# A two-layer MoE and ternary-FFN kernel on one Trainium2 core: rounding of the second layer's weights and the collect tables moved to GpSimd, VectorE's chains issued step by step

## The reference, cut to what matters

```python
def reference(x, ...):                       # x: 128 x 32 x 256, taken as 4096 tokens of 256
    h = x W^T + (x A_b^T) B_b^T * s_b        # adapter b chosen for each sample of 32 tokens
    scores = sigmoid(h gate_w^T)             # 8 experts, the two best of each token
    routed = sum over both: expert(h * score), expert(v) = (silu(v w1^T) * (v w3^T)) w2^T
    x = x + routed + shared expert(h)
    y = per-sample 32 x 32 mix of x          # a weight gathered by a condition index
    z = hbitlinear(relu(hbitlinear(y, w_up))^2, w_down)
    return x + z
# hbitlinear(v, w): v by a Walsh-Hadamard transform, rounded to 8 bits by row;
# w rounded to -1, 0, 1 times s, where s is the mean of |w|
```

## Time and profile before

| | us |
|---|---|
| median of 3 runs | 354.83 (352.88 to 356.35) |
| the profiled execution, its time | 355.2 |
| its span, first to last instruction | 353.4 |
| PE busy | 320.1 (91%) |
| DVE busy | 277.7 (79%) |
| ACT busy | 224.3 (63%) |
| POOL busy | 207.7 (59%) |

### The profile page before, as it was taken

How to read it: one execution, slowest core, us unless ns; L and a number is a source line. 1 busy time by engine, 2 the same in 40 slices (tenths; PEclk the granted TensorE clock), 3 DMA queues, 4 the chain that set the end, 5 groups by cost and what they waited for, 6 DMA issues and landing times.

```text
span 353.4 us, 8743 instructions
## 1 busy us (share of the span) xinstructions
PE 320.1 (91%) x2564; PEld 296.6 (84%) x2564; DVE 277.7 (79%) x732; ACT 224.3 (63%) x529; POOL 207.7 (59%) x211
## 2 busy tenths in 40 slices
PE   7999999799998999699999998999996889997785
PEld 6799988699888999598999988999985878885684
DVE  2788899988998888986545458778969898886796
ACT  4664331323445375457776767899788697896793
POOL 1100889889998899900002878888548888884000
PEclk9999999699999999999999999999999999999999
DMA  6982559162287578458497996868947458574004
GB/s 190 376 286 86 167 203 304 66 204 72 77 256 227 163 261 272 154 154 254 147 287 244 220 253 110 174 119 174 205 99 130 68 77 165 93 125 89 2 1 150
DMA packets 54092, 59.23 MB, mean 168 GB/s; under 512 B 9888, under 2 KB 48032, under 8 KB 54048
## 3 DMA queue, kind: packets, MB, share of 16 engines
q1 hardware_dynamic: 41040, 41.01, 37.9%
q0 software_dynamic: 12432, 17.57, 24.1%
q10 hardware_dynamic: 576, 0.10, 0.2%
HBM read 33.06 MB, written 25.59 MB: 166 GB/s over the span
## 4 chain that ended last, share of the span: by engine, by line
PE 30%; issue 11%; POOL 7%; DVE 7%; ACT 4%; DMA 2%; ACTq 0%; POOLq 0%; DVEq 0%
PE UP L1295 9%; POOL X L1395 7%; PE DN L1349 5%; PE TR L1262 3%; PE LB L1647 2%; PE HT L1327 2%; PE AUX L1647 1%; DMA X<-ys,POSY 1%; PE AUX L1461 1%; PE AUX L1506 1%; DVE XSL L1280 1%; DVE ST L1655 1%; PE UP L868 1%; PE AUX L1585 1%; ACT YS L1360 1%
## 5 line engine op out<-in xcount | busy, mean ns | idle before, releaser
L1395 POOL DMA_INDIRECT X<-ys,POSY x64 | 103.0, 1610 | 69.5 <-DMA ys<-YS 49.5
L1043 POOL DMA_INDIRECT hs<-ZF,POS x64 | 66.5, 1038 | 10.5 <-issue 9.9
L1042 POOL MEMSET PACE<- 128x512 f32 x64 | 35.1, 548 | 21.1 <-DVE POS L1031 21.0
L1295 PE MATMUL UP<-WH,XSH 128*128 x142 | 43.2, 304 | 0.5 <-issue 0.5
L1295 PE MATMUL UP<-WH,XSL 128*128 x142 | 39.9, 281 | 0.0
L1295 PE MATMUL UP<-WL,XSH 128*128 x142 | 39.8, 280 | 0.0
L1280 DVE TENSOR_TENSOR XSL<-TR,XSH 128x512 fp32r<-128x512 f32 (+1 forms) x36 | 24.4, 679 | 12.9 <-ACT XSH L1275 12.6
L1309 ACT ACTIVATE T<-UP,SCOL 128x128 f32<-128x128 f32 x71 | 22.4, 370 | 10.4 <-PE UP L1295 8.0
L1295 PEld LDWEIGHTS UP<-WH,XSH 128*128 128x128 f32 x142 | 26.8, 188 | 1.9 <-issue 1.3
L809 PE MATMUL AUX<-WH,ZR 128*128 128x264 f32 x128 | 26.6, 302 | 1.7 <-ACT ZF L832 1.1
L1275 ACT ACTIVATE XSH<-TR 128x512 fp32r<-128x512 f32 (+1 forms) x36 | 21.3, 592 | 8.9 <-PE TR L1262 8.5
(11 more groups left out here) (327 smaller groups left out, 999.1 us busy)
## 6 DMA issues: line engine op xcount, KB each, us to landing
ys<-YS SPq DMA_DIRECT2D x42, 256.0 KB, 3.4
XIN<-hs SPq DMA_DIRECT2D x71, 132.0 KB
X<-in_x SPq DMA_DIRECT2D x8, 512.0 KB, 6.8
out<-X SPq DMA_DIRECT2D x16, 256.0 KB, 2.9
X<-in_WE SPq DMA_DIRECT2D x8, 384.0 KB, 9.6
ZF<-in_xT SPq DMA_DIRECT2D x4, 512.0 KB, 4.4
XR<-in_xT SPq DMA_DIRECT2D x4, 512.0 KB, 7.9
hs<-ZERO SPq DMA_DIRECT2D x8, 132.0 KB
```

Of the source, the lines that this page charges most:

```text
L1042: e.memset(PACE[:, :], 0.0).then_inc(S["pac"], 1)
L1043: e.indirect_dma_start(hs, bass.IndirectOffsetOnAxis(ap=POS[:, k, t0 + t:t0 + t + 1], axis=0), HT[:, slot + t, :], None).then_inc(s_st[b % ...
L1295: mm = e.matmul(UP[s % 2][:, c * 256:c * 256 + 256], v[:, r % 2, k, c * P:(c + 1) * P], w[:, cols], start=(n == 0), stop=(n == 5))
L1395: e.indirect_dma_start(X1[:, tt, :], None, ys[p], bass.IndirectOffsetOnAxis(ap=POSY[:, k, tt:tt + 1], axis=0), compute_op=ALU.add).then_in ...
```

## The change

Four things are changed.

1. **Rounding on GpSimd.** `ternary` leaves VectorE. Its six steps on 128x1024 are cut in halves, which gives twelve steps on 128x512, and these stand in place of twelve of GpSimd's `PACE` memsets, at scatters 16 to 27. The four tiny steps stay on VectorE as `scales`. Loads and copies that reuse the weights' tiles wait for twelve steps, not six.
2. **Collect tables on GpSimd.** `home` leaves VectorE for GpSimd, after the last scatter, and its comparison is written with subtract, add, max and min, its sum over 16 columns with four halving adds. The first collect waits for both tables.
3. **Single steps.** VectorE's chains (`nonzero`, `sigmoid`, `top1`, `top2`, `place`, `first_count` and so on, `stats1`, `stats2`) are no longer one piece each but one piece a step: each step waits for what it reads, and `TIME` may set other work between them.
4. **Loads.** The constants come in one DMA, the condition indices on SP, `RAWB` after the adapter indices, and some loads of `x` and of expert weights later.

`TIME` is new throughout, for example:

```diff
-    "collect": [
-        183.4459, 185.3059, 187.1659, 192.7459, 196.4659, 200.1859, 202.0459, 209.4859, 211.3459, 213.2059,
+    "collect": [
+        177.6604, 179.5204, 181.3804, 186.9604, 190.6804, 194.4004, 196.2604, 198.1204, 207.4204, 209.2804,
```

The core of the rest:

```diff
+TERNARY_AT = 16
...
-            n = 0
-            for raw, q, c in ((WUR, WU, 4), (WDR, WD, 5)):
+        def ternary(e, i):
+            raw = (XFLAT[:, 0:2 * HID], YFLAT)[i // 2 % 2][:, i % 2 * HID:i % 2 * HID + HID]
+            q = (WU[:, :, :], WD[:, :, :])[i // 2 % 2].rearrange("p a b -> p (a b)")[:, i % 2 * HID:i % 2 * HID + HID]
+            c = 4 + i // 2 % 2
+            if i < 4:
+                e.wait_ge(S["sw"], 2)
                 e.tensor_scalar(raw, raw, SW[:, c:c + 1], MAGIC, ALU.mult, ALU.add).then_inc(S["wt"], 1)
-                e.wait_ge(S["wt"], n + 1)
+            elif i < 8:
+                e.wait_ge(S["wt"], i - 3)
                 e.tensor_scalar(raw, raw, MAGIC, 1.0, ALU.subtract, ALU.min).then_inc(S["wt"], 1)
-                e.wait_ge(S["wt"], n + 2)
-                e.tensor_scalar(q[:, :, :], raw, -1.0, None, ALU.max).then_inc(S["wt"], 1)
-                n += 3
-        at("vector", "ternary", 0, ternary)
+            else:
+                e.wait_ge(S["wt"], i - 3)
+                e.tensor_scalar(q, raw, -1.0, None, ALU.max).then_inc(S["wt"], 1)
...
             def scatter(e, t, k):
...
-                if k_th > 0:
-                    e.wait_ge(S["pac"], k_th)
-                e.memset(PACE[:, :], 0.0).then_inc(S["pac"], 1)
+                if TERNARY_AT <= k_th < TERNARY_AT + 12:
+                    ternary(e, k_th - TERNARY_AT)
+                else:
+                    cleared = k_th - (12 if k_th > TERNARY_AT else 0)
+                    if cleared > 0:
+                        e.wait_ge(S["pac"], cleared)
+                    e.memset(PACE[:, :], 0.0).then_inc(S["pac"], 1)
...
             def home(e):
+                e.wait_ge(S["pl"], 6 * GROUPS_OF[SEGMENTS[p]])
+                e.wait_ge(S["pt"], LINES_DONE[p])
+                e.wait_ge(S["pac"], 8 * NBLK - 12)
...
-                over = OVER[:, 0:2 * NE * n].rearrange("p (t i) -> p t i", i=2 * NE)
+                over = PACE[:, :].rearrange("p (k t i) -> p k t i", k=2, i=2 * NE)
+                for k in range(2):
+                    link(e, e.tensor_tensor(over[:, k], POSF[:, k, lo:hi].unsqueeze(2).broadcast_to([P, n, 2 * NE]), edge,
+                                            ALU.subtract))
+                link(e, e.tensor_scalar(PACE[:, :], PACE[:, :], 1.0, 0.0, ALU.add, ALU.max))
+                link(e, e.tensor_scalar(PACE[:, :], PACE[:, :], 1.0, None, ALU.min))
                 for k in range(2):
-                    link(e, e.tensor_tensor(over, edge, POSF[:, k, lo:hi].unsqueeze(2).broadcast_to([P, n, 2 * NE]), ALU.is_le))
-                    link(e, e.tensor_tensor(over, over, step, ALU.mult))
-                    link(e, e.tensor_reduce(SUMS[:, k, 0:n], over, AX.X, ALU.add))
-                e.tensor_tensor(POSY[:, :, lo:hi], POSF[:, :, lo:hi], SUMS[:, :, 0:n], ALU.add).then_inc(S["hom"], 1)
-            at("vector", "home", p, home)
+                    link(e, e.tensor_tensor(over[:, k], over[:, k], step, ALU.mult))
+                flat = PACE[:, :].rearrange("p (t i) -> p t i", i=2 * NE)
+                for w in (8, 4, 2, 1):
+                    link(e, e.tensor_tensor(flat[:, :, 0:w], flat[:, :, 0:w], flat[:, :, w:2 * w], ALU.add))
+                link(e, e.tensor_tensor(SUMS[:, :, 0:n], POSF[:, :, lo:hi], over[:, :, :, 0], ALU.add))
+                e.tensor_copy(POSY[:, :, lo:hi], SUMS[:, :, 0:n]).then_inc(S["hom"], 1)
+            at("gpsimd", "home", p, home)
...
                         if t == 0:
-                            e.wait_ge(S["hom"], p + 1)
+                            e.wait_ge(S["hom"], PARTS)
...
-            at("vector", "stats1", b, stats1)
+            for i in range(3):
+                at("vector", "stats1", b, lambda e, i=i: stats1(e, i), i)
```

More of the change, by code:

```diff
@@ new lines, in plan_route, with pick @@
+            for i in range(4):
+                at("vector", "sigmoid", g, lambda e, i=i: sigmoid(e, i), i)
+            def pick(e, j, sc, base, i):
+                e.wait_ge(S["gch"], before + 6 + 6 * j + i)
+                if i == 0:
+                    ins = e.tensor_reduce(g4(2 * j), r(sc), AX.X, ALU.max)
+                elif i == 1:
+                    ins = e.tensor_tensor(r(base), r(sc), c(2 * j), ALU.is_equal)
+                elif i == 2:
+                    ins = e.tensor_tensor(r(base + 1), r(base), w8, ALU.mult)
+                elif i == 3:
+                    ins = e.tensor_reduce(g4(2 * j + 1), r(base + 1), AX.X, ALU.max)
+                elif i == 4:
+                    ins = e.tensor_tensor(r(base + 2), r(base + 1), c(2 * j + 1), ALU.is_equal)
+                elif j == 0:
+                    ins = e.scalar_tensor_tensor(out=f(7), in0=f(6), scalar=-4.0, in1=f(3), op0=ALU.mult, op1=ALU.add)
+                else:
+                    ins = e.tensor_tensor(MCB[:, cols], f(6), f(10), ALU.add)
+                ins.then_inc(S["gch"], 1)
@@ new lines, in adapter_moe_quant_ffn, with whole, running @@
+        LINES_DONE = [COUNT_0 + STEPS_C * i + 11 for i in range(PARTS)]
+        HOME_LINKS = [16 * i for i in range(PARTS)]
+        def whole(e, i, out, rows, bias):
+            if i == 0:
+                return e.tensor_scalar(SM[:, 4, :], rows, bias, 1.0 / P, ALU.add, ALU.mult)
+            if i == 1:
+                return e.tensor_scalar(SM[:, 5, :], SM[:, 4, :], MAGIC, None, ALU.add)
+            return e.tensor_scalar(out, SM[:, 5, :], MAGIC, float(P), ALU.subtract, ALU.mult)
+        def running(e, i, length, k):
+            if i == 0:
+                return e.tensor_copy(PB[:, k, 0, NE:2 * NE], length)
+            d = (1, 2, 4)[i - 1]
+            return e.tensor_tensor(PB[:, k, i, NE:2 * NE], PB[:, k, i - 1, NE:2 * NE], PB[:, k, i - 1, NE - d:2 * NE - d],
+                                   ALU.add)
@@ new lines, in plan_first, with first_tables @@
+            for i in range(10):
+                at("vector", "first_count", 0, lambda e, i=i: first_count(e, i), i)
+            def first_tables(e, i):
+                if i < 4:
+                    e.wait_ge(S["pt"], 10 + i)
+                    spread(e, i, PARTS, n, filled[:, NE:2 * NE], jump).then_inc(S["pt"], 1)
+                else:
+                    tables(e, i - 4, 14, 0, n, EXF[:, PARTS, 0:n], ROWF[:, PARTS, 0:n], line[:, 0:1])
+            for i in range(9):
+                at("vector", "first_tables", 0, lambda e, i=i: first_tables(e, i), i)
@@ L1166, in plan_segment @@
[L1166 to L1175 removed]
+                e.tensor_copy(TAIL[:, :], end).then_inc(S["tl"], 1)
@@ new lines, in plan_segment, with last_tables @@
+            for i in range(7):
+                at("vector", "jumps", c, lambda e, i=i: jumps(e, i), i)
+            def last_tables(e, i):
+                number, rows, part, digit = EXF[:, 0, 0:n], ROWF[:, 0, 0:n], EXF[:, PARTS + 1, 0:n], EXF[:, PARTS + 2, 0:n]
+                first = COUNT_0 + STEPS_C * PARTS
+                if i < 4:
+                    e.wait_ge(S["pt"], first + i)
+                if i == 0:
+                    e.tensor_scalar(part, EXF[:, 0, 0:n], float(NE), -float(NE), ALU.is_ge, ALU.mult).then_inc(S["pt"], 1)
+                elif i == 1:
+                    e.tensor_tensor(digit, part, EXF[:, 1, 0:n], ALU.add).then_inc(S["pt"], 1)
+                elif i == 2:
+                    e.tensor_tensor(number, number, digit, ALU.add).then_inc(S["pt"], 1)
+                elif i == 3:
+                    e.tensor_tensor(rows, rows, ROWF[:, 1, 0:n], ALU.add).then_inc(S["pt"], 1)
+                else:
+                    tables(e, i - 4, first + 4, 1, n, number, rows, LINE[:, 0, 0:1])
@@ L1176, in plan_segment @@
             if c == PARTS - 1:
-                at("vector", "last_tables", 0, last_tables)
+                for i in range(9):
+                    at("vector", "last_tables", 0, lambda e, i=i: last_tables(e, i), i)
             def tails(e):
```

539 lines of the change are left out of this document (296 added, 243 removed), and 258 rows, old and new, of the table TIME.

## The result

The changed kernel takes **362.64 us** (median of 4 runs, 362.03 to 365.26) against 354.4 us (352.88 to 356.35): a ratio of **1.0244**, 95% interval 1.0172 to 1.0315. It is slower by 8.2 us. 357.8 was forecast, 0.8% slower than before, with a range of 349.3 to 363.3: the time lies inside the range, near its upper end and near the time of rival B (362.3). The profiled execution has a span of 360.0 us, 6.6 us more than before.

What follows compares the result with a forecast made beforehand. Phase 2's start was taken to bound the kernel. The scatter chain gains 3.3 us and pays S = 10.5; phase 2 starts 4.8 us later with 1.8 us less work: +3.0, 358.2 profiled, 357.8 us median, range 349.3 to 363.3.

Steps and rivals of the forecast that it cites:

- rival B: GpSimd's queue becomes the bound: reload and fillers delay scatters, last scatter gates phase 2; S = 15, 362.3 us; chance 0.35.
- Phase 2's start sets the time: From phase 2's first transpose to the last pair TensorE is busy 95.1 of 98.6 us, so its start sets the time.
- Part 1: VectorE without rounding: 5.9 us leave ahead of group 2's chain; TensorE and ScalarE reach block 7 5.8 us earlier, at 97.1.
- The chain's gain of 3.3 us: GpSimd's scatter chain: 2.0 us of rounding's delay and 1.27 us of waits for POS go away.
- L, the reload: GpSimd library reload ahead of the first rounding step: 6 us, ends 0 and 9.6.
- F, the dearer filler: Rounding steps in GpSimd's fillers cost 0.29 us more than a memset, times 12: 3.5 us, ends 0 and 5.
- C: Clashes of GpSimd's new fillers with VectorE: three of a third of a microsecond, 1 us; ends 0 and 3.
- S: Price paid by the scatter chain, L + F + C = 10.5 us, ends 0 and 17.6; the end shifts by S - 7.5.
- Where S goes: ScalarE waits about 7 us at block 7; phase 2's loads, at 163.2, come last, behind TensorE's 158.5 or 161.9.
- A: Rival: the reload on GpSimd is cheap, S = 3, shift -4.5, 350.3 us; sign: gap on GpSimd missing; chance 0.20.
- Part 3: Collect tables on GpSimd after the last filler: 0, with a cover of 35 us before the first collect.
- Part 4: Single steps and loads: 0, with -1 to +1 in the last 32 us, behind the last collect.

Runs made afterwards that it cites:

- forms: round_on_vector with twelve different GpSimd steps on 128x512 in place of the memsets at scatters 16 to 27; mult and add took 0.63 us, others 1.53 to 2.34.
- steps_alone: Changed kernel with rounding and collect tables both back on VectorE, single steps and new order kept: 362.24 us, ratio 1.0195.
- round_on_vector: Changed kernel with the twelve rounding steps back on VectorE and all 64 fillers memsets again; tables stay on GpSimd: 353.68 us, ratio 0.9964.
- round_alone: Kernel before with only the twelve rounding steps moved to GpSimd, at scatters 16 to 27; scales stay on VectorE: 367.22 us, ratio 1.0343.
- two_forms: Changed kernel with rounding's second step written as mult and add, its third as max and min, same result: 360.94 us, ratio 1.0179.

## Why the prediction was right and wrong

**Phase 2's start sets the time: right.** The tail took as long as before: from the 33rd collect, the first that waits for the last pair, to the end of the span 92.8 us (360.0 less 267.24) against 92.9 (353.4 less 260.46). Over the kernels with the new order and the tables on GpSimd, the time moves with the first load of phase 2. The changed kernel's first and 33rd collect:

```profile
197.44 1.68 POOL L1536 DMA_INDIRECT X<-ys,POSY  x1 [16.01 <-issue]
...
267.24 1.54 POOL L1536 DMA_INDIRECT X<-ys,POSY  x1 [8.94 <-DMA ys<-YS]
```

**Part 1: right in sum.** The full clock in 66 to 72 came; the wait of 1.8 us near 62 shrank to 0.8, and one of 1.9 us arose at group 3's ranks near 89. ScalarE was ready for block 7 at 97.70; 97.1 was forecast.

**The chain's gain of 3.3 us: too high.** Scatter 16's filler began at 64.86 in place of 66.15, 1.3 us earlier. Two early DMAs took 1.41 and 1.60 us where before they took 1.02 and 1.10, and a third 1.47. The prediction also misread its row of 1.82 us. That DMA (50.55) begins beside a low-part step, which stays in the changed kernel, and not beside the rounding, which begins at 51.84; and scatter 16's DMA is as long with no rounding near it. Rows of the kernel before (the second DMA's neighbour is the L758 of the earlier trace rows):

```profile
50.32 1.21 DVE L758 TENSOR_TENSOR ZR<-ZF,ZR 128x1024 fp32r<-128x1024 f32 x1
```

```profile
66.83 1.83 POOL L1043 DMA_INDIRECT hs<-ZF,POS  x1 [0.16 <-issue]
```

The rounding itself held the chain up by 1.2 us: a memset of 0.96 in place of 0.54 and three DMAs of 1.23 in place of 0.97. The other 0.85 was the low-part step's, and could not be gained.

**L, the reload: wrong.** 6 us were taken; the gap in the rows is 0.14 us, where the next rounding step has 0.04. The first step (1.12 against 0.70) and the DMA behind it (1.79) are long for another reason, a low-part step of VectorE beside both:

```profile
65.43 1.63 DVE L793 TENSOR_TENSOR ZR<-XR,ZR 128x1024 fp32r<-128x1024 f32 x1
```

The run `forms` has the same pair of 1.12 and 1.78 us behind its second step, beside the same VectorE step, with no reload between the first step and the second; and before, scatter 16's DMA took 1.83. So the reload shows no cost beyond the gap of 0.14 us. The Trainium skill's page "GPSIMD Engine Reference", section "2.1 Instruction dispatch", by which about 6 us would stand there, does not agree with this trace. The ends 0 to 9.6 held, at the lower one.

**F, the dearer filler: wrong, and the term that decided.** 0.29 us each, 3.5 in all, ends 0 to 5, from memset rows. Measured: the twelve steps sum to 17.5 us, twelve memsets to 6.5, so 11.0. The step that failed is the bound "0.96 if they add up": it took the cost of an element from a memset and assumed that an arithmetic step reads and writes at that rate, whatever it computes. By form it is 0.7, 1.95 or 1.6 us. No row of before shows a TENSOR_SCALAR of that size on GpSimd, so the upper bound had nothing under it. The section "4.1 Engine selection" of the Trainium skill's page "GPSIMD Engine Reference" advises VectorE for elementwise work and calls one-input steps on GpSimd "roughly line-rate"; here that agrees for `mult, add` (0.7 us against VectorE's 0.5) and not for the others (1.5 to 2 against 0.4 to 0.8).

**C: inside its ends**, 1.6 us in DMAs and 0.7 in gaps, 2.3 against the 1 forecast, with ends 0 to 3. Of the 1.6, 1.1 stand in two DMAs beside the low-part step L793 (1.79 and 1.30 in place of 0.98).

**S = 13.3, forecast 10.5 within 0 to 17.6.** L too high by 6 and F too low by 7.5 all but cancelled, so it is partly luck that the time came out inside the range. The shift by the rule S - 7.5 would be 5.8; it was 6.6 in the profiled execution and 8.2 between medians. S is past 11, where rival B was said to decide, and GpSimd's queue did become the bound, but by another price than B's, which had it from the reload, and with scatter 31 and not the last scatter on the chain that ended last. B's sign, phase 2 past 166, did not come (164.88). A's sign, no gap on GpSimd, did, with S = 13.3 in place of A's 3.

**Where S goes: the places right, the last link wrong.** Last filler 154.8 forecast, 157.42 measured; first transpose 163.2 and 164.88; scatter 31 landed at 103.9 and 106.4; ScalarE's idle time 7 and 8.8 us with the scatter's DMA as releaser; the low clock behind it, which the prediction had as an alternative. "The loads come last" is the step that failed here: the transpose did not wait for them. TensorE came last, behind scatter 31 and the low clock, the route that the prediction put at 161.9. With 2.5 us for the later scatter 31 that route gives 164.4. The prediction also left out that scatter 31 gates phase 1's tile loads, which came 10.0 us later. The 1.8 us of work moved ahead of phase 2 gave nothing: phase 2 took 99.3 us with 5.0 us of idle time in it, before 99.0 with 3.5. What the added idle time waits for was not followed up.

**Part 3, tables at 0: right for the cover, wrong as a price.** They ran from 159.11 to 180.5 us, under a cover that ended at 197.44; the forecast for their end was 187. But off VectorE they are worth 8.5 us in the new order, and in the old order they cost 4. The prediction took VectorE's 8 us of tables as hidden, though the chain that ended last before runs through them, and on GpSimd it asked only who waits for the tables, not what is queued behind them.

**Part 4 at 0, -1 to +1: wrong by itself.** Single steps, loads and order with the tables on VectorE are 2% slower (`steps_alone`). Parts 3 and 4 together give -0.4% (`round_on_vector`), so the two errors cancel too: in these runs neither part has a price of its own. The change of the loads was not tried apart.

## What to carry to other kernels

- A filler on a queue that paces a critical chain is not free room: each slot's excess is multiplied by the number of slots. Twelve slots took 33.4 us with the rounding and 35.1 us with three memsets each, in place of 20.
- When a scatter's landing is what others wait for, follow each of its waiters. Here scatter 31 held up both ScalarE's copies and phase 1's loads, and the chain that ended last went through it, though the last scatter was thought to be the gate.
- A step that the trace has never shown on an engine has no upper bound from another operation's rows. Measure the form itself, with its operations, before pricing twelve of them.
- When work goes behind the last item of a queue, list what stands behind it there, and whose queue waits for that: here SyncE, and through it the loads of the next pairs.

## What the runs showed of the hardware that was not expected

- GpSimd's TENSOR_SCALAR on 128x512 fp32 takes 0.63 to 0.84 us for `mult` with `add` in either order, with constants or a column; 1.5 us for `min`, `max`, `add` or greater-than alone (1.5 to 1.7 for `max` with bf16 output); 1.8 for `subtract` alone (one row); and 1.9 to 2.1 for `subtract, min`; `add, min`; `max, min`; `subtract, mult`; `mult, subtract`; `add, add` (one `subtract, min` in `round_alone` took 2.76, beside such a VectorE step as the next point has). `mult` alone took 1.86 and 2.34 and `mult, min` 2.21, each with a VectorE step on 128x1024 beside part of it. One operation alone can be dearer than the quick pair.
- A step of VectorE on 128x1024 with two inputs in SBUF lengthens what GpSimd does beside it: a scatter's DMA takes 1.8 to 2.1 us in place of 0.97 (66.83 and 83.05 before, 66.15 in the changed kernel, 89.87 in `round_alone`; also 50.55 before, where the rounding begins beside its end), and the quick pair 1.1 to 2.1 us in place of 0.7 (64.86 in the changed kernel, 69.93 in `forms`, 66.60 in `two_forms`, 64.52 in `round_alone`).
- The row of the program that reloads GpSimd's library shows a gap of 0.14 us here, ahead of the first rounding step, and no other cost.
- Scatters every 1.47 us in place of 1.68 went with a phase 1 slower by 25 us; why stays open.
